# A four-layer GNN and FFN on one core: the two convolutions gather by slot into a ring of 32, from a table of three bf16 parts

## What is computed

```
h = x @ W
dinv = rsqrt(deg)                      # deg counts a node's incoming edges and its self-loop
msg = h[src] * (dinv[src] * dinv[dst])[:, None]
out = segment_sum(msg, dst) + b
x = x + relu(out)
```

## Time and profile before

| | |
|---|---|
| runs | 3408.43, 3417.91, 3418.81 us; median 3417.91 |
| the profiled execution | 3414.29 us, its span 3412.6 us |
| PE / DVE / POOL / ACT busy | 66% / 51% / 40% / 11% of the span |
| a1, first gather to last accumulation | 502.6 to 1100.1 us |
| a2, first gather to last accumulation | 1409.3 to 2002.1 us |
| a3, first to last gather | 2486.6 to 3118.3 us |

### The profile page before, as it was taken

How to read it: one execution, slowest core, us unless ns; L and a number is a source line. 1 busy time by engine, 2 the same in 40 slices (tenths; PEclk the granted TensorE clock), 3 DMA queues, 4 the chain that set the end, 5 groups by cost and what they waited for, 6 DMA issues and landing times. The chain is left out here.

```text
span 3412.6 us, 35808 instructions
## 1 busy us (share of the span) xinstructions
PE 2259.6 (66%) x8719; PEld 1605.6 (47%) x8720; DVE 1748.6 (51%) x4031; ACT 388.2 (11%) x835; POOL 1376.5 (40%) x1300
## 2 busy tenths in 40 slices
PE   4108974455556788545555559999867777775597
PEld 3006753233324345323333337777655655564376
DVE  7457763344335774534343453333466666666443
ACT  1002220000001220100000022222211111110122
POOL 1820006767673120367676710000066666664100
PEclk9558986767667897777576669999977777777799
DMA  4201023333331000433333300000033333331000
GB/s 118 60 26 30 0 63 97 97 93 95 93 97 49 0 0 7 131 94 93 93 94 95 93 25 1 0 0 0 24 94 90 91 90 85 86 89 51 28 15 22
DMA packets 104762, 205.70 MB, mean 60 GB/s; under 512 B 33704, under 2 KB 63323, under 8 KB 104572
## 3 DMA queue, kind: packets, MB, share of 16 engines
q0 software_dynamic: 60304, 169.70, 18.4%
q1 hardware_dynamic: 44396, 35.29, 3.5%
HBM read 187.91 MB, written 16.73 MB: 60 GB/s over the span
## 5 line engine op out<-in xcount | busy, mean ns | idle before, releaser
L393 POOL DMA_INDIRECT BIG<-table,CSTB x784 | 794.5, 1013 | 796.4 <-DMA table<-ACC 458.5
L535 PE MATMUL PB<-BIG,OH 128*128 x1664 | 630.1, 531 | 558.7 <-issue 355.1
L535 PEld LDWEIGHTS PB<-BIG,OH 128*128 128x128 f32 x1664 | 396.5, 261 | 792.3 <-issue 732.4
L381 POOL DMA_INDIRECT BIG<-table,SRCI x416 | 428.6, 1030 | 715.4 <-DMA table<-ACC 512.4
L1204 DVE TENSOR_TENSOR ACC<-ACC,PB 128x256 f32 x832 | 350.1, 421 | 652.9 <-issue 241.5
L745 PE MATMUL PB<-BIG,WA 128*128 128x264 f32 x832 | 295.6, 504 | 126.7 <-DVE BIG L1477 54.7
L745 PEld LDWEIGHTS PB<-BIG,WA 128*128 128x128 f32 x832 | 187.3, 243 | 192.3 <-issue 81.6
L1507 DVE TENSOR_TENSOR ACC<-ACC,PB 128x264 f32 x416 | 176.9, 425 | 152.3 <-remote 83.9
L1406 DVE SCALAR_TENSOR_TENSOR X<-PB,SMALL,X 128x256 f32 (+1 forms) x200 | 96.7, 484 | 220.8 <-PE PB L678 220.8
L1477 DVE TENSOR_TENSOR BIG<-BIG 128x256 f32<-128x256 f32 x416 | 156.7, 418 | 76.5 <-ACT BIG L911 53.9
L669 PE MATMUL PB<-XT,WA 128*128 128x320 f32 x640 | 187.2, 449 | 7.5 <-DVE X L1413 7.5
(11 more groups left out here) (337 smaller groups left out, 2370.7 us busy)
## 6 DMA issues: line engine op xcount, KB each, us to landing
table<-ACC SPq DMA_DIRECT2D x20, 660.0 KB, 3.4
BIG<-table,CSTB POOLq DMA_INDIRECT x784
BIG<-table,SRCI POOLq DMA_INDIRECT x416
X<-in_x SPq DMA_DIRECT2D x1, 3072.0 KB
out<-X SPq DMA_DIRECT2D x4, 640.0 KB
WA<-in_L_ffn_w SPq DMA_DIRECT2D x1, 2048.0 KB
WB<-in_L_ffn_w SPq DMA_DIRECT2D x1, 2048.0 KB
BIG<-wtab SPq DMA_DIRECT2D x1, 1600.0 KB, 6.2
```

The costliest lines, as they stand in the source:

```text
L381: g.indirect_dma_start(out=G[:, k * ROW:(k + 1) * ROW], out_offset=None, in_=table, in_offset=bass.IndirectOffsetOnAxis(ap=SRCI[:, n:n + 1 ...
L393: g.indirect_dma_start(out=GT[:, k * ROW:(k + 1) * ROW], out_offset=None, in_=table, in_offset=bass.IndirectOffsetOnAxis(ap=TSRC[:, n:n + ...
L535: pe.matmul(PB[k][:, 0:width], OH[:, ((q % 2) * GRP + k) * P:((q % 2) * GRP + k + 1) * P], GT[:, ds(t, width)], start=True, stop=True).the ...
```

## The change

- Layers 1 and 2 gather by slot too: 416 indirect DMAs each, indices `SRCI`, into a ring of 32 places, from a new HBM tensor `parts`. A row of `parts` has 768 bf16 (1536 bytes, where a row of `table` has 1056): a high, a middle and a low part of 256 each, whose sum is the fp32 row. The ring's wait, for all three graph steps, is now slots done >= n - 24 (with `BODY` = 32 added to both sides), which for a ring of 32 is exact.
- PE multiplies the slot's bf16 one-hot with the three parts, one after the other into the same `PB[k]`. It loads no registers. Its loop and DVE's take four groups a turn, 13 turns.
- DVE writes the one-hots as bf16 (inputs still fp32).
- The project stage of g1 and g2 makes the parts (`project_parts`): ACT copies the row to bf16 (high), DVE subtracts it from the row (rest, in two places `REST1` of `SW`), ACT copies the rest to bf16 (middle), DVE subtracts that (low, written as bf16). SP stores 983 KB a chunk in place of 676 KB, and waits for the low parts.
- At the start the edge tiles' own indices (`tile_src`, `TSRC`, `TROW`) and the arithmetic for them are gone, and one gather with a zero index (`IDX`) ahead of everything on POOL. SP no longer waits for a2 before it loads the attention vectors of layer 3.

```diff
@@ gpsimd
-            g.memset(IDX[:, :], 0).then_inc(sem("idx_zero"), 1)
-            g.wait_ge(sem("idx_zero"), 1)
-            g.indirect_dma_start(out=BIG[:, 0:D], out_offset=None, in_=a["x"],
-                                 in_offset=bass.IndirectOffsetOnAxis(ap=IDX[:, :], axis=0)).then_inc(sem("first_gather"), 16)
-            g.wait_ge(sem("first_gather"), 16)
...
-            def gather_slots(tb, st):
+            def gather_slots(tb, st, ring, width, rows):
+                if st == "a1":
+                    g.wait_ge(sem("slots_ready"), 1)
                 g.wait_ge(sem("table_stored"), (GNNS.index(tb) + 1) * NC * 16)
                 for n in range(SLOTS):
                     q = n // GRP % NG
                     if n % GRP == 0:
-                        g.wait_ge(sem(f"{st}_mm"), BODY + n - 2 * GRP)
+                        g.wait_ge(sem(f"{st}_mm"), n + GRP)
                     k = n % BODY
-                    g.indirect_dma_start(out=G[:, k * ROW:(k + 1) * ROW], out_offset=None, in_=table,
+                    g.indirect_dma_start(out=ring[:, k * width:(k + 1) * width], out_offset=None, in_=rows,
                                          in_offset=bass.IndirectOffsetOnAxis(ap=SRCI[:, n:n + 1], axis=0)).then_inc(sem(f"{st}_in{q}"), 16)
-            gather_tiles("g1", "a1")
+            gather_slots("g1", "a1", GT, W3, parts)
...
@@ tensor
             def sum_slots(st, width):
                 pe.sem_inc(sem(f"{st}_mm"), BODY)
-                        pe.wait_ge(sem(f"{st}_oh"), i * TG + q + 1)
-                        pe.load(regs, TROW[0:1, ds(n0, GRP)])
+                with pe.Fori(0, TURNS) as i:
+                    for q in range(NG):
+                        pe.wait_ge(sem(f"{st}_in{q}"), 16 * GRP * (i + 1))
+                        pe.wait_ge(sem(f"{st}_oh"), i * NG + q + 1)
                         for k in range(GRP):
-                            t = pe.snap(regs[k], min_val=0, max_val=(RING - 1) * ROW)
-                            pe.wait_ge(sem(f"{st}_acc"), BODY + n0 + k + 1 - GRP)
-                            pe.matmul(PB[k][:, 0:width], OH[:, ((q % 2) * GRP + k) * P:((q % 2) * GRP + k + 1) * P],
-                                      GT[:, ds(t, width)], start=True, stop=True).then_inc(sem(f"{st}_mm"), 1)
+                            pe.wait_ge(sem(f"{st}_acc"), BODY + i * BODY + q * GRP + k + 1 - GRP)
+                            for part in range(3):
+                                mm = pe.matmul(PB[k][:, 0:width], OHB[:, ((q % 2) * GRP + k) * P:((q % 2) * GRP + k + 1) * P],
+                                               GT[:, (q * GRP + k) * W3 + part * D:(q * GRP + k) * W3 + part * D + width], start=(part == 0), stop=(part == 2))
+                            mm.then_inc(sem(f"{st}_mm"), 1)
...
@@ scalar
+            def project_parts(st):
+                for n in range(NT):
+                    act.wait_ge(sem(f"{st}_mm"), AHEAD + n + 1 - CH)
+                    to_xt(st, n // CH, n % CH)
+                    if n > 1:
+                        parts_of(st, n - 2)
+                parts_of(st, NT - 2)
+                parts_of(st, NT - 1)
+            def parts_of(st, n):
+                act.wait_ge(sem("rows"), rows_before(st) + AHEAD + n + 1)
+                act.activation(SPLIT[:, n * W3:n * W3 + D], tile(ACC, n, D, ROW), ACT.Copy).then_inc(sem(f"{st}_hi"), 1)
+                act.wait_ge(sem(f"{st}_rest"), n + 1)
+                act.activation(SPLIT[:, n * W3 + D:n * W3 + 2 * D], REST1[:, (n % 2) * D:(n % 2 + 1) * D], ACT.Copy).then_inc(sem(f"{st}_mid"), 1)
...
@@ vector
+            def project_parts(st):
+                def row(t):
+                    v.wait_ge(sem(f"{st}_mm"), AHEAD + t + 1)
+                    v.tensor_scalar(tile(ACC, t, D, ROW), PB[2 + t % CH][:, 0:D], DINV[:, t:t + 1], None, ALU.mult).then_inc(sem("rows"), 1)
+                def rest(t):
+                    v.wait_ge(sem("rows"), rows_before(st) + AHEAD + t + 1)
+                    v.wait_ge(sem(f"{st}_hi"), t + 1)
+                    v.tensor_tensor(REST1[:, (t % 2) * D:(t % 2 + 1) * D], tile(ACC, t, D, ROW), SPLIT[:, t * W3:t * W3 + D], ALU.subtract).then_inc(sem(f"{st}_rest"), 1)
+                def low(t):
+                    v.wait_ge(sem(f"{st}_rest"), t + 1)
+                    v.wait_ge(sem(f"{st}_mid"), t + 1)
+                    v.tensor_tensor(SPLIT[:, t * W3 + 2 * D:t * W3 + 3 * D], REST1[:, (t % 2) * D:(t % 2 + 1) * D], SPLIT[:, t * W3 + D:t * W3 + 2 * D],
+                                    ALU.subtract).then_inc(sem(f"{st}_lo"), 1)
...
+                for t in range(NT + 2):
+                    if t + 3 < NT:
+                        ln_apply(st, (t + 3) // CH, (t + 3) % CH, False)
+                    if t < NT:
+                        row(t)
+                    if 0 <= t - 2:
+                        low(t - 2)
+                    if 0 <= t - 1 < NT:
+                        rest(t - 1)
```

More of the change, by code:

```diff
@@ L141, in build @@
         table = nc.dram_tensor("table", (NT * P, ROW), F32, kind="Internal").ap()
+        parts = nc.dram_tensor("parts", (NT * P, W3), BF16, kind="Internal").ap()
         wtab = nc.dram_tensor("wtab", (1, NT * P), F32, kind="Internal").ap()
         G = BIG[:, 0:BODY * ROW]
[L145 to L148, removed]
+        GT = BIG[:, 0:BODY * W3 // 2].bitcast(BF16)
+        SPLIT = BIG[:, 0:NT * W3 // 2].bitcast(BF16)
+        REST1 = SW[:, 0:2 * D]
+        OHB = OH[:, 0:GRP * P].bitcast(BF16)
         RANKROW = BIG[:, 5120:5120 + NT * P]
@@ L250, in _, with store_parts @@
             store_table("g0")
+            def store_parts(st):
+                for c in range(NC):
+                    sp.wait_ge(sem(f"{st}_lo"), (c + 1) * CH)
+                    sp.dma_start(parts[c * CW:(c + 1) * CW, :].rearrange("(t p) c -> p t c", p=P),
+                                 SPLIT[:, c * CH * W3:(c + 1) * CH * W3].rearrange("p (t c) -> p t c", c=W3)).then_inc(sem("table_stored"), 16)
+                    sp.wait_ge(sem("table_stored"), (GNNS.index(st) * NC + c + 1) * 16)
             sp.dma_start(WA[:, 0:KB * 1024].rearrange("p (b c) -> p b c", b=KB), a["L0_ffn_w1"].rearrange("(b p) c -> p b c", p=P)).then_inc(sem("ld_f0"), 16)
@@ L405, in _ @@
                     g.tensor_tensor(WSUM, WSUM, SW[:, j * 512:(j + 1) * 512], ALU.add).then_inc(sem("t1_wsum"), 1)
-            gather_tiles("g2", "a2")
-            gather_slots("g3", "a3")
+            gather_slots("g2", "a2", GT, W3, parts)
+            gather_slots("g3", "a3", G, ROW, table)
             with g.Fori(0, NC) as c:
@@ L521, in sum_slots @@
                 pe.sem_inc(sem(f"{st}_mm"), BODY)
[L522 to L529, removed]
-                        pe.wait_ge(sem(f"{st}_oh"), i * TG + q + 1)
-                        pe.load(regs, TROW[0:1, ds(n0, GRP)])
-                        for k in range(GRP):
-                            t = pe.snap(regs[k], min_val=0, max_val=(RING - 1) * ROW)
-                            pe.wait_ge(sem(f"{st}_acc"), BODY + n0 + k + 1 - GRP)
-                            pe.matmul(PB[k][:, 0:width], OH[:, ((q % 2) * GRP + k) * P:((q % 2) * GRP + k + 1) * P],
-                                      GT[:, ds(t, width)], start=True, stop=True).then_inc(sem(f"{st}_mm"), 1)
-                with pe.Fori(0, S_GROUPS // TG) as i:
-                    body(i, TG, TG)
-                body(S_GROUPS // TG, S_GROUPS % TG, T_GROUPS % TG)
-                for r in regs:
-                    pe.free_register(r)
+                with pe.Fori(0, TURNS) as i:
+                    for q in range(NG):
+                        pe.wait_ge(sem(f"{st}_in{q}"), 16 * GRP * (i + 1))
+                        pe.wait_ge(sem(f"{st}_oh"), i * NG + q + 1)
+                        for k in range(GRP):
+                            pe.wait_ge(sem(f"{st}_acc"), BODY + i * BODY + q * GRP + k + 1 - GRP)
[3 more added lines that the diff above has]
+                            mm.then_inc(sem(f"{st}_mm"), 1)
             pe.wait_ge(sem("ld_wg"), 16)
@@ L839, in _ @@
             ln_root("g1")
-            project("g1")
+            project_parts("g1")
             def slices(st):
@@ L875, in _ @@
             ln_root("g2")
-            project("g2")
+            project_parts("g2")
             relus("a2")
@@ L1026, in _ @@
             attention_columns(lambda b, k: WG[:, b * GW + D + 4 * k:b * GW + D + 4 * k + 4], CSTB[:, 0:D], CSTB[:, D:2 * D], 4, "g0_weights")
+            def project_parts(st):
[11 more added lines that the diff above has]
+                                    ALU.subtract).then_inc(sem(f"{st}_lo"), 1)
+                for t in range(3):
+                    ln_apply(st, 0, t, False)
+                for t in range(NT + 2):
[7 more added lines that the diff above has]
+                        rest(t - 1)
             def project(st, width, scaled):
@@ L1204, in body @@
                             v.tensor_tensor(dst, dst, PB[k][:, 0:width], ALU.add).then_inc(sem(f"{st}_acc"), 1)
```

(7 more changed lines are left out.)

47 lines of the change are left out of this document (6 added, 41 removed).

## The result

The changed kernel took 3508.2 us (median of four runs, 3502.4 to 3509.9), the kernel before 3418.0: a ratio of 1.0267, interval 1.0246 to 1.0289. The forecast was 3487 (3376 to 3530). The profiled execution has a span of 3508.2 us, 95.6 more than before.

What follows compares the result with a forecast made beforehand. No engine was full; in a1 and a2 POOL's gathers, with pauses, set 1.449 and 1.442 us each. Gathers +30, project stages +46 and setup -3.4 made +73 on the profiled 3414.3, so 3487 us, range 3376 to 3530 (8 in 10).

Steps and rivals of the forecast that it cites:

- Step 1: Gathers of a1 and a2: 24 more each at the old pace, with a shorter tail; +14.1 and +16.1, together +30 us.
- slow stretches: In the sums: times when DVE's accumulations come 1.4 to 3.5 us apart with nothing busy; some fifteen a convolution, cause unknown.
- The 3.7 us that I gave the lead: Start of a1 and a2: POOL's larger lead in slots saves about one pause, taken at 3.7 us in each.
- Step 2: Gathers of a1 and a2: 1.45 times the bytes a row cost nothing; upper bound +91 us a convolution.
- step 3: PE in a1 and a2: three bf16 matmuls a slot, at most 1.16 us, hidden by POOL's pace; 0, at most +13 each.
- step 4: DVE's one-hots in a1 and a2: bf16 saves nothing, and a one-hot still delays a gather, by 0.8 us.
- Step 5: Project stage of g1 and g2: a loop through ACT sets 2.0 us a tile for 1.24; +23 each, +46 us together.
- Step 6: Setup at the start: PE's index work goes and two DVE casts come; -3.4 us.
- Step 7: Gathers of a3: POOL may lead by 8 more slots, which brings nothing; 0, bounds 0 to +8 us.
- A: Rival, a1 and a2: the lead, larger early on, halves POOL's pauses, 55 to 27 us a convolution; 3432 us, chance 0.22.
- B: Rival, a1 and a2: slow stretches go with PE's register loads and shorter loop, POOL alone the pace; 3376 us, chance 0.20.
- D: Rival, a1 and a2: more gather traffic worsens the slow stretches, 1.50 us a gather, +21 each; 3529 us, chance 0.13.

Runs made afterwards that it cites:

- lead16: Changed kernel with a1's and a2's gathers waiting for slots done >= n - 16 in place of n - 24: 3510.7 us, 1.0257 of the kernel before.
- hi_only: Changed kernel storing and gathering only the high part (512-byte rows, one bf16 matmul a slot): 3545.3 us, ratio 1.0358 to the kernel before; repeat 3543.3, 1.0314.
- slots_fp32: Changed kernel without the parts (fp32 table rows, one fp32 matmul a slot, old project stage): 3468.6 us, ratio 1.0146 to the kernel before; repeat 3482.0, 1.0149.
- bank7: Changed kernel with a chunk's fifth tile transposed through bank 7 in g1's and g2's project stage: 3232.6 us, ratio 1.0068 to the kernel before, series without slow stretches.
- a3_ring: Kernel before with only a3's wait changed, to slots done >= n - 24 in place of n - 16: 3438.8 us, 1.0035 of the kernel before.
- dve_unrolled: Changed kernel with DVE's loop over a1's and a2's slots written out: 3241.5 us, ratio 1.0100 to the kernel before, series without slow stretches.
- before_unrolled: Kernel before with DVE's loop over a1's and a2's slots written out: 3200.0 us, ratio 0.9971 to the kernel before, series without slow stretches.

## Why the prediction was right, point by point

*Step 1, the gathers.* Right while the slow stretches occur. From first to last start a1 and a2 took 597.7 and 598.0 us, where the sum has 597.6 and 594.9. The sum left out the last gather itself (1.75 and 0.94 us), and it put the tail at 14 where its own 24 x 0.62 is 14.9; the tails are 15.8 and 15.7. So the term came out at +39.6 for +30: some 3 us each from a2's gathers, the last gathers and the tails. The pauses are 49 and 47 us, about what the sum left of them, but the lead has no part in that: lead16, with 8 slots less, has 49 and 48. The 3.7 us that I gave the lead are within the scatter, 42 to 56 us over the kernels with stretches other than hi_only. What I hadn't seen: the term hangs on the slow stretches. With them the pace is 1.44 a gather in both kernels, and 24 gathers cost 34.6 us less the 12 to 14 of the shorter tail; without them the term is 0 and +6 us.

*Step 2, bytes; step 3, PE; step 4, one-hots.* Right: nothing. slots_fp32 and the changed kernel have the same a1 and a2, with 1056 and 1536 bytes a row and 2 and 3 matmul records a slot. PE is busy 244.8 us in a1. The bf16 one-hot is as long as the fp32 one, 1.22 us, and still delays gathers, as the one at 1119.43 (1.76 us), beside a one-hot that began at 1119.15. In a1, from 530 us on, no gather clear of one takes over 0.96 us, and about half of those that start under one take 1.6 us or more.

*Step 5, the project stage.* The size is right (+44 for +46; slots_fp32 makes it 41), the mechanism is not, and the agreement is luck. The loop rest, middle part, `XT`, high part isn't 1.97 but about 1.5: the rest started at 479.26 and the high part ends at 480.70 (its start, 480.29, and 0.41), with 0.05 to the next rest. ACT's copies take 0.41 and start 0.26 to 0.33 apart, where I had priced them one behind another and from L800's 0.51, a copy with `DINV` as an operand more. DVE's own four instructions, 1.6 us, are the pace within a chunk. What made up the 2.0 was a wait that I had read past: at a chunk's first tile PE waits for the copy to `XT` of the tile just before, not of the one before that, as tiles 4 and 0 share a bank. ACT's copy now stands behind the middle part of an earlier tile, so PE stands idle there (1.96 us at 480.45) and one row a seam comes 1.7 to 2.8 us late. bank7 takes that wait away, and the mean is 1.62. Two errors of opposite sign met. Behind the last row I had put 3.2 us, though the terms named add up to some 2.1; it measures 3.1. The store landed in 4.1 us and DVE waited 4.14 where I had 5.0.

*Step 6, the setup.* -2.8 for -3.4.

*Step 7, a3.* Wrong, and the largest miss of a single term: 0, with 0 to +8 as bounds. a3_ring measures +11 for the wait alone, and the traces of the changed kernel have 10.6 in the gathers and 6.5 behind them. That the larger lead brings nothing was right; that it costs nothing holds only without slow stretches.

*The rivals.* A, that the lead halves the pauses, falls with 49 and 47 us for 52 and 48, and with lead16. B hung on the stretches going with PE's register loads or its shorter loop. They did not go. Its price was also high: the sums without stretches take 540 and 542 us (dve_unrolled), where I had 554.6. D, that more traffic makes them worse, falls with hi_only: less traffic, longer pauses. By the rule that I had weighed, a fetch and a stall when a branch goes out of the window (the Trainium skill, "Runtime: NRT & Kernel Launch", Instruction fetch mechanics), the shorter loop bodies would have helped. No run here shows that: the packets of instructions are 23 and 37 for 25 and 37 (writing out DVE's loop in before_unrolled takes the 37 to 59, so fetches do show in them), and the pauses stayed.

*The range.* The forecast's own range, 3463 to 3515, doesn't follow from the terms beside it: with -20 its lower end is 3467, and with +20, +26 and +5 its upper end 3538. The measured time is in either.

So the net is: +44 project, +40 sums, +17 around a3, -3 setup, -3 between the stages. The forecast's 73 became 96, by a3's 17 and the sums' 10, less 2 of the project stage and 3 between.

What stays open: what makes DVE's sequencer slow. The runs show that it isn't the kernel alone (the same kernel before took 3207 and 3429 us on one chip), and that the bytes, the lead and DVE's instruction count don't set it. In the traces it occurs only while POOL gathers, and it ends once POOL pauses: in each of the 28 pauses of over 0.3 us in a1 and a2 of the changed kernel, one or two slow additions start and then no more. What else on the machine takes part can't be told from here.

## What to carry to other kernels

Before costing a stage by its own steps, read the waits at the seams of a loop: a wait that is one tile stricter at a chunk's first tile cost PE no idle time over 0.6 us here while ACT had slack, and 1.7 to 2.8 us a chunk once ACT got more to do. When a producer's pace is kept by a stall of unknown cause, measure the kernel before more than once: a term worked out from that pace (here +40 us in the sums) can vanish with the stall (here down to +6). And a split into parts that makes matmuls cheaper buys nothing where PE isn't waited for, while the engines that make the parts stand on the path.

## What the hardware showed that I had not expected

- One and the same kernel took 3207 and 3429 us in two series on one chip, recorded some twelve minutes apart, each series steady within 1.2%. The difference is 6%. Between the traces of before and before_unrolled it lies whole in the three sums (58, 57 and 104 of 219 us), in stretches in which DVE's additions come multiples of 0.70 us apart, 2.8 to 8.4, where 0.62 is the rule.
- An indirect gather of 128 rows takes 0.94 to 0.95 us on POOL (the median) at 512, 1056 and 1536 bytes a row.
- With a third of PE's matmuls in a1 and a2 the granted clock stayed at 0.50, and the kernel was 30 to 37 us slower, though PE was busy a quarter of the time. That the clock is the cause isn't shown.
